# A four-layer kernel on one core: the first stage's closing in another order, middle row tiles written out, bfloat16 bias parts

## The reference

```python
x = x + time_mixing(layernorm(x))      # 16 heads of 8, a scan over the tokens: S = d*S + k v
x = x + top1_ffn(layernorm(x))         # 8 experts 128 -> 512 -> 128 with ReLU, one expert for each token
x = x + memory(layernorm(x))           # holographic memory, below
x = x + top4_moe(layernorm(x))         # 32 experts 128 -> 64 -> 128 and a shared one

# memory: quaternions, 32 of 4 components in 128 channels
keys = (x @ Wk.T + bk).reshape(B, L, 32, 4);  keys = keys / max(norm(keys), 1e-12)
values = (x @ Wv.T + bv).reshape(B, L, 32, 4)
memory = cumsum(quat_mul(values, keys), axis=1)
retrieved = quat_mul(memory, conj(keys)) / sqrt(positions)
return x + (normalize(retrieved) * ln_g + ln_b) @ Wo.T + bo
```

## Time and profile before

| | |
|---|---|
| median of 3 runs | 786.58 us (785.86 to 790.19) |
| the profiled execution | 793.46 us, of which 791.7 from first to last instruction |
| mean granted TensorE clock | 0.977 of full |
| PE busy | 723.0 us (91%) |
| DVE, ACT, POOL busy | 595.1, 485.0, 490.5 us |

### The profile page before, as it was taken

How to read it: one execution, slowest core, us unless ns; L and a number is a source line. 1 busy time by engine, 2 the same in 40 slices (tenths; PEclk the granted TensorE clock), 3 DMA queues, 4 the chain that set the end, 5 groups by cost and what they waited for, 6 DMA issues and landing times.

```text
span 791.7 us, 14395 instructions
## 1 busy us (share of the span) xinstructions
PE 723.0 (91%) x4028; PEld 546.7 (69%) x4029; DVE 595.1 (75%) x1387; ACT 485.0 (61%) x1045; POOL 490.5 (62%) x498
## 2 busy tenths in 40 slices
PE   4999999999868789788999898999999999999996
PEld 2445555455438689777887876787878787878784
DVE  3699999999975645547888777686868686868673
ACT  3677767664535357466566566666666666666553
POOL 3687768787753544447877846555556666555663
PEclk9999999999968999899999999999999999999998
DMA  8800000000011256221000018373636464636550
GB/s 254 253 0 1 2 1 13 9 8 15 14 34 48 55 164 163 68 60 33 14 1 1 2 36 181 72 158 81 150 86 144 95 136 99 131 87 145 112 117 14
DMA packets 38298, 60.48 MB, mean 76 GB/s; under 512 B 3808, under 2 KB 17760, under 8 KB 37840
## 3 DMA queue, kind: packets, MB, share of 16 engines
q1 hardware_dynamic: 35952, 54.94, 29.3%
q0 software_dynamic: 2272, 4.67, 1.7%
HBM read 51.32 MB, written 8.28 MB: 75 GB/s over the span
## 4 chain that ended last, share of the span: by engine, by line
PE 43%; DVE 6%; ACT 2%; issue 2%; DMA 1%; SPq 0%; POOLq 0%; DVEq 0%; POOL 0%; ACTq 0%
PE c_r L1964 3%; PE c_m L1983 3%; PE c_m L1984 3%; PE c_m L1985 3%; PE c_m L1948 3%; PE c_v L1983 2%; PE c_r L2033 2%; PE c_k L1983 2%; PE c_r L2035 2%; PE c_r L2032 2%; PE c_v L1985 2%; PE c_v L1984 2%; PE c_k L1984 2%; PE c_k L1985 2%; PE c_o L2035 2%
## 5 line engine op out<-in xcount | busy, mean ns | idle before, releaser
L2527 POOL TENSOR_TENSOR d_hid_lo<-c_bound,d_hid_hi 128x512 fp32r<-128x512 f32 x136 | 175.5, 1292 | 128.4 <-ACT d_hid_hi L2431 127.0
L2431 ACT ACTIVATE d_hid_hi<-c_bound 128x512 fp32r<-128x512 f32 x136 | 85.4, 628 | 28.1 <-DVE c_bound L2292 26.5
L1471 POOL TENSOR_TENSOR ducts_and_memory_weights<-a_r,state_and_wide 128x512 f32<-128x512 f32 x64 | 75.4, 1189 | 26.7 <-DVE state_and_wide L871 22.2
L871 DVE TENSOR_TENSOR_SCAN state_and_wide<-a_decay,state_and_wide,a_vb 128x512 f32<-128x512 f32 x64 | 80.9, 1266 | 0.4 <-issue 0.3
L2280 DVE TENSOR_TENSOR c_m<-c_bound,c_m 128x512 f32<-128x512 f32 x64 | 44.3, 692 | 23.9 <-PE c_m L1985 17.4
L2280 DVE TENSOR_TENSOR c_v<-c_bound,c_v 128x512 f32<-128x512 f32 x64 | 44.3, 693 | 22.9 <-PE c_v L1985 16.9
L1983 PE MATMUL c_m<-d_x_hi,d_hi 128*128 128x512 f32 x136 | 55.5, 408 | 1.8 <-DVE c_bound L2292 1.8
L2421 ACT ACTIVATE c_bound<-c_m 128x512 f32<-128x512 f32 x60 | 35.8, 596 | 33.3 <-PE c_m L1985 32.8
L2421 ACT ACTIVATE c_bound<-c_k 128x512 f32<-128x512 f32 x60 | 35.8, 597 | 32.8 <-PE c_k L1985 32.2
L1984 PE MATMUL c_m<-d_x_lo,d_hi 128*128 128x512 f32 x136 | 53.9, 396 | 0.0
L1985 PE MATMUL c_m<-d_x_hi,d_lo 128*128 128x512 f32 x136 | 53.9, 396 | 0.0
(11 more groups left out here) (394 smaller groups left out, 2148.3 us busy)
## 6 DMA issues: line engine op xcount, KB each, us to landing
state_and_wide<-pair_weights SPq DMA_DIRECT2D x62, 512.0 KB, 11.7
b_w<-in_w SPq DMA_DIRECT2D x2, 2048.0 KB, 11.6
state_and_wide<-in_moe SPq DMA_DIRECT2D x16, 204.0 KB
a_xf<-rows_in SPq DMA_DIRECT2D x39, 64.5 KB
state_and_wide<-results SPq DMA_DIRECT2D x8, 256.0 KB, 3.1
out<-c_read SPq DMA_DIRECT2D x8, 256.0 KB, 2.4
a_weights<-in_mixing SPq DMA_DIRECT2D x1, 1077.0 KB, 6.6
state_and_wide<-pair_weights SPq DMA_DIRECT2D x2, 384.0 KB, 6.1
```

Of the source, the lines that this page charges most:

```text
L871: dve.tensor_tensor_scan(state[:, j, seq_cols(h, 1)], decay[:, h, :], vb[j % 3][:, :], first, ALU.mult, ALU.add).then_inc(scan_ready, 1)
L1471: pool.tensor_tensor(rs[:, j, :], rr[:, h, :], state[:, j, seq_cols(h, 0)], ALU.mult).then_inc(rs_ready, 1)
L2431: act.activation(hid_hi[:, n % HALVES, :], hidden[:, r, :], ACT.Copy).then_inc(hi_ready, 1)
L2527: pool.tensor_tensor(hid_lo[:, n % HALVES, :], hidden[:, r, :], hid_hi[:, n % HALVES, :].bitcast(F32), ALU.subtract).then_inc(lo_ready, 1)
```

## The change

Four things are altered.

1. `closing` has another order on TensorE, VectorE, ScalarE and GpSimd. The calls are the same.
2. The loop of 16 rows is gone. Rows 12 to 26 (`MIDDLE_ROWS` = 15) are written out, and the written-out rows with steps beside them are the last 12 instead of the last 11. `FIRST_ROWS` is 27 in place of 28. The weights still come in 16 pieces.
3. The steps beside the last rows are given by a table for each engine. ScalarE's normalization of tile 0 is in two halves, and some of its steps come behind the last row.
4. The bias of the projections is held in three bfloat16 parts, on partitions 0, 32 and 64 of 96. In `project` the wait for the turned input stands behind the bias matmul.

```diff
-LOOPED_ROWS = 16
+MIDDLE_ROWS = 15
+PIECES = 16
-FIRST_ROWS = EARLY_ROWS + LOOPED_ROWS
+FIRST_ROWS = EARLY_ROWS + MIDDLE_ROWS
...
-            bodies = LOOPED_ROWS // 8
-            with engine.Fori(0, bodies) as b:
-                for n in range(STORES):
-                    row(STORES * b + EARLY_ROWS + n, (EARLY_ROWS + n) % STORES, b + (EARLY_ROWS + n) // STORES)
+            for k in range(EARLY_ROWS, EARLY_ROWS + MIDDLE_ROWS):
+                row(k, k % STORES, k // STORES)
...
+            def project(bank, name, weight, turned, turned_ready, count):
                 pe.matmul(bank[:, :].rearrange("p (s c) -> p s c", s=SUB), ones[:, :], bias_row(name), start=True, stop=False)
+                pe.wait_ge(turned_ready, count)
...
     (each call of project had its wait for xt_ready or normedt_ready in front of it)
...
-            "bias": ctx.enter_context(nc.sbuf_tensor("bias", [2 * LO_ROW, len(BIASES) * P], F32R)),
-            "ones": ctx.enter_context(nc.sbuf_tensor("ones", [2 * LO_ROW, P], F32R)),
+            "bias": ctx.enter_context(nc.sbuf_tensor("bias", [BIAS_ROWS, len(BIASES) * P], BF16)),
+            "ones": ctx.enter_context(nc.sbuf_tensor("ones", [BIAS_ROWS, P], BF16)),
...
                 if n == 1:
                     dve.wait_ge(bias_rounded, 1)
+                    rest(second, bias_rounded)
+                    rest(third, bias_rounded)
+                if n == 2:
+                    dve.wait_ge(bias_rounded, 3)
+                    rounded_part(second, bias_rounded)
+                    rounded_part(third, bias_rounded)
+                if n == 3:
+                    dve.wait_ge(bias_rounded, 5)
+                    rest(third, bias_rounded)
+                    dve.wait_ge(bias_rounded, 6)
+                    rounded_part(third, bias_ready)
...
-        BESIDE = ((), (), ((0, 3), (0, 4)), ((0, 5), (0, 6), (1, 3), (1, 4)), ((0, 9), (1, 5)), ((0, 12), (1, 6)),
-                  (0, 1), (2, 3), (5,), (6, 7), ((1, 9),))
+                start(norm, ahead, row, {7: [("norm", 0, 12)], 9: [("ahead", 0, 0)]})                      # PE
+                start(norm, ahead, row, {4: [("norm", 0, 3), ("norm", 0, 4)], 5: [("norm", 0, 5), ("norm", 1, 3)],
+                                         6: [("norm", 1, 4)], 7: [("norm", 1, 5)], 10: [("ahead", 0, 2)],
+                                         11: [("ahead", 0, 5), ("ahead", 0, 6)]})                          # DVE
+                start(norm, ahead, row, {6: [("norm", 0, 9)], 7: [("norm", 0, 10)], 8: [("norm", 0, 12)],
+                                         10: [("ahead", 0, 1)], 11: [("ahead", 0, 3)]})                    # ACT
+                start(norm, ahead, row, {5: [("norm", 0, 6)], 7: [("norm", 1, 6)]})                        # POOL
...
             last_rows["act"](beside)
+            ahead(0, 0, 5)
+            ahead(0, 0, 7)
+            norm(1, 1, 9)
             norm(1, 1, 12)
```

More of the change, by code:

```diff
@@ L432, in emit @@
             def emit(beside):
-                for k in range(EARLY_ROWS + LOOPED_ROWS, ROW_TILES):
+                for k in range(EARLY_ROWS + MIDDLE_ROWS, ROW_TILES):
                     row(k, k % STORES, k // STORES)
-                    beside(k - EARLY_ROWS - LOOPED_ROWS)
+                    beside(k - EARLY_ROWS - MIDDLE_ROWS)
                 if end:
@@ L1137, in closing @@
                 e0 = bias_hidden(0, 0, 0)
+                e1 = bias_hidden(1, 1, 0)
+                tail(7, 1, 11)
+                look(6, 0, 8)
+                pick(5, 1, 13)
+                pick(5, 1, 14)
+                e2 = bias_hidden(2, 2, 0)
+                look(6, 0, 9)
                 tail(7, 1, 13)
-                pick(6, 0, 13)
-                pick(6, 0, 14)
-                e1 = bias_hidden(1, 1, 0)
+                bias_out(0, 0, e0)
+                e3 = bias_hidden(3, 3, 0)
                 tail(7, 1, 15)
@@ L1144, in closing @@
                 look(7, 1, 2)
-                e2 = bias_hidden(2, 2, 0)
-                look(7, 1, 8)
-                look(7, 1, 9)
-                bias_out(0, 0, e0)
-                e3 = bias_hidden(3, 3, 0)
                 bias_out(1, 1, e1)
                 e4 = bias_hidden(4, 4, 0)
+                look(7, 1, 8)
+                pick(6, 0, 8)
+                look(7, 1, 9)
+                pick(6, 0, 9)
+                pick(6, 0, 10)
+                pick(6, 0, 11)
                 bias_out(2, 2, e2)
+                pick(6, 0, 13)
+                pick(6, 0, 14)
                 e5 = bias_hidden(5, 5, 0)
+                bias_out(3, 3, e3)
+                e6 = bias_hidden(6, 6, 0)
+                bias_out(4, 4, e4)
                 pick(7, 1, 8)
@@ L1365, in closing @@
             def closing():
+                pick(5, 1, 5)
                 act.wait_ge(early_loaded, 16 * (len(early) + 4))
@@ L1516, in closing @@
                 send_one(7, 3)
-                give_back(3, 3)
                 give_back(4, 4)
@@ L1713, in bias_row @@
             n = BIASES.index(name)
-            return bias[:, n * P:(n + 1) * P].unsqueeze(1).broadcast_to([2 * LO_ROW, SUB, P])
+            return bias[:, n * P:(n + 1) * P].unsqueeze(1).broadcast_to([BIAS_ROWS, SUB, P])
         def spread_component(ap):
@@ L1793, in split_cols, with start @@
             return n, slice(part * width, (part + 1) * width)
-        BESIDE = ((), (), ((0, 3), (0, 4)), ((0, 5), (0, 6), (1, 3), (1, 4)), ((0, 9), (1, 5)), ((0, 12), (1, 6)),
-                  (0, 1), (2, 3), (5,), (6, 7), ((1, 9),))
-        def start(norm, ahead, row):
-            for each in BESIDE[row]:
-                if isinstance(each, tuple):
-                    norm(each[0], each[0] % 2, each[1])
+        def start(norm, ahead, row, places):
+            for stage, i, step in places.get(row, ()):
+                if stage == "norm":
+                    norm(i, i % 2, step)
                 else:
-                    ahead(0, 0, each)
+                    ahead(i, i % 2, step)
         def weave(engine, norm, ahead, main, tail, look, route, unit, end):
@@ L2073, in beside @@
                     pe.wait_ge(loaded["taken"], 1)
-                start(norm, ahead, row)
+                start(norm, ahead, row, {7: [("norm", 0, 12)], 9: [("ahead", 0, 0)]})
             last_rows["pe"](beside)
@@ L2322, in norm @@
             def norm(i, h, step):
-                if step == 9:
+                if step in (9, 10) and (step == 9 or i == 0):
                     act.wait_ge(shift_ready, i + 1)
@@ L2326, in norm @@
                     need(act, kept_ready, i - 1)
-                    for s in range(SUB):
+                    for s in range(SUB) if i else (0, 1) if step == 9 else (2, 3):
                         a = act.activation(xn[:, h, s, :], x_tok[:, SUB * i + s, :], ACT.Identity,
                                            bias=shift[:, s:s + 1], scale=rstd[:, s:s + 1])
-                    a.then_inc(xn_ready, 1)
+                    if i or step == 10:
+                        a.then_inc(xn_ready, 1)
                 if step == 12:
@@ L2443, in beside @@
                     act.wait_ge(loaded["taken"], 1)
-                start(norm, ahead, row)
+                start(norm, ahead, row, {6: [("norm", 0, 9)], 7: [("norm", 0, 10)], 8: [("norm", 0, 12)],
+                                         10: [("ahead", 0, 1)], 11: [("ahead", 0, 3)]})
             last_rows["act"](beside)
+            ahead(0, 0, 5)
+            ahead(0, 0, 7)
+            norm(1, 1, 9)
             norm(1, 1, 12)
@@ L2534, in beside @@
                 if row == 3:
-                    pool.wait_ge(bias_ready, 1)
+                    pool.wait_ge(bias_rounded, 1)
                     pool.wait_ge(loaded["taken"], 1)
-                start(norm, ahead, row)
+                start(norm, ahead, row, {5: [("norm", 0, 6)], 7: [("norm", 1, 6)]})
             last_rows["pool"](beside)
@@ L2618, in packed_quaternions @@
     part["wo"][:] = t["Wo"].T
-    for row in (0, LO_ROW):
+    for row in range(0, BIAS_ROWS, PART_ROWS):
         part["bias"][row] = np.concatenate([t[name] for name in BIASES])
```

186 lines of the change are left out of this document (85 added, 101 removed).

## The result

The changed kernel takes 775.52 us (773.95 to 777.01) where the kernel before took 786.58: 0.9848 of it, interval 0.9821 to 0.9875. Timed twice more beside the kernel before it gave 0.9844 (0.9828 to 0.9860) and 0.9869 (0.9851 to 0.9887). The forecast was 764 with a range of 757 to 775. The sign was right and the size was half: 10.8 to 12.7 us of the 22.7.

The account below looks back on a forecast made before the run. TensorE was taken to bound the looped rows and memory stage, with waits of about 8 to 9 us in each stretch beside the rows. Gains 7 + 3.3 + 6.3 + 6.1 = 22.7 us off 786.58 gave 764 us, range 757 to 775.

Parts of the forecast that it names:

- closing: End of the first stage: reordering brings row 12's bias about 6 us behind the plan, not 15.2; 7 us gained.
- rows written out: Rows 12 to 26 without the loop: 1.90 us each on TensorE, 28.5 us instead of 31.76; 3.3 us gained.
- head: Last rows with the memory stage's start: VectorE's 2.27 us wait for returned results goes; 6.3 us gained, bounds 3 and 9.
- memory stage: Three bias matmuls per tile get cheaper or leave the chain; 6.1 us gained, bounds 3.0 and 8.7.
- I take zero: Closing: the plan itself was assumed to come neither earlier nor later; bounds -2 (gain) and +5 us.
- Rival 1: Closing gives little, 1 us, as the plan slips behind three expands or stalls return; 770 us, chance 0.17.
- value term: Memory stage, value projection: a cheaper bias matmul saves 0.30 us in each of seven tiles.
- output term: Memory stage, output projection: the bias matmul moves into TensorE's wait for normed_t, saving 0.50 us, counted eight times.
- Does TensorE stay the bound? It does: Memory stage: VectorE's work, GpSimd's read and TensorE's reads make 13.3 us per tile, below the 14.0 forecast.
- rival 2: Written-out rows: instructions come late, at most three stalls, +10 us on the forecast, 774 us; chance 0.08.
- rival 3: The 96-row bias matmul is no cheaper and the head's wait moves: memory part 3, head 3, 770 us; chance 0.08.
- Rivals 4 and 5: 4: waits re-form everywhere, 785 us, chance 0.04. 5: lower clock stays through written-out rows, 792.5 us, chance 0.03.

Follow-up runs that it names:

- middle_only: The kernel before with its 16 looped rows written out and nothing else; 784.18 us, 0.9970 of before.
- closing_back: The changed kernel with the old order of the closing on all four engines; 778.36 us, 0.9889 of before.
- after_again: The changed kernel unaltered, run once more for a trace at the ordinary TensorE clock; 774.16 us.
- after_third: The changed kernel unaltered, run once more on the chip of the third group; 776.61 us, 0.9869 of before.
- head_back: The changed kernel with the steps beside the last rows at their old places, FIRST_ROWS still 27; 794.04 us, 1.0026 of before, on the second group's chip.
- bound_first: The changed kernel with VectorE's two products (bound) ahead of the addition got in the memory stage; 770.3 us, 0.9784 of before.
- norm_early: The changed kernel with VectorE's results' addition and statistics of memory tiles 3 to 7 half a tile earlier; 792.73 us, 0.9999 of before, second group's chip.

## Why the prediction was right in sign and wrong in size

| term | forecast | measured |
|---|---|---|
| closing | 7 | 1.0 alone, 1.75 in company |
| rows written out | 3.3 | 2.65 alone; 1.7 and 3.1 in the traces (31.76 to 30.10 and 28.66) |
| head | 6.3 | 4.8 to 6.0 in the traces (38.70 to 33.88 and 32.71); no run timed it alone |
| memory stage | 6.1 | 1.5 by the medians, 2.9 in the traces |

**Closing: the step that failed is "I take zero" for the plan, and the 15.2 us before it.** That row 12 would come about 6 us behind the plan was right (6.70, 7.64). But the new order makes the plan later: it ends at 265.8 and 266.4, in the old order, on chips of the same sort, at 261.8, 262.9 and 262.7. I had looked for that at `tail(7, 14)` behind three expands, and it isn't there: the last addition to x is at 244.55 against 243.99 in middle_only. The loss comes behind it, 16.1 us from there to the plan's start in place of 12.7 (13.6 in closing_back). Read from the order of time (no run tested it), two places make up most of the difference. The turning of tile 7's rows (`pick(7)` 4) stands on TensorE behind `contract(3)` and `expand(6)` and starts at 252.62, 1.85 us after they are ready, where in middle_only it is 0.63. `bias_hidden(8)` and `bias_out(5)`, which I had counted as work taken from behind the plan, stand before it: VectorE is done with tile 7's index at 259.16 and starts the plan at 260.69, where in middle_only it starts it at once. `count_all`, now behind `expand(8)`, ends at 258.5 and holds up nothing. What is taken from one side of a fixed piece is put on the other. And the 15.2 us held stalls of that chip: the order itself gives 12.0 to 12.3. From there to the 6.7 to 7.9 with the new order are 4 to 5 us, and the plan, 3 to 4.6 us later, takes most of them. Rival 1 named this outcome (closing 1 us) with the wrong place; its 770 is not the result, since a second term failed too.

**Rows: right where they run free.** In after_again six steps from 291.25 to 302.62 are 1.90 us each and the clock is 1.00, but the rows before them take longer (one step, where TensorE waits for a row's load, is 3.20), so that the 15 steps are 30.10 us; in after_third and middle_only they are 28.66, close to the 28.5 of the forecast. Alone the part gives 2.65 and not 3.3.

**Head: right, place by place in the trace.** The wait for the results went, that for `shift` is 2.53, TensorE's 2.66. The bias parts held the addition to 10.2 us behind row 27, where I had 8.6, and ScalarE's start came at 16.5 for 15.4; later steps gave it back. (The forecast's terms for the aggregates add up to 11.6, where it has 12.0.) How much of it is the new places stays open between 1.4 and 3.6 us, by head_back.

**Memory stage: the value term was right, the output term 0.43 for 0.50, and waits took back 0.47.** The value bias is 0.22 us to the next start and the eight behind it 0.89: 1.11 us from the bias to `c_m`, where the order in time of before has 0.42 and 0.99, so 0.30. The Trainium skill's TensorEngine Tiling (Array Packing), Key Properties, has the engine drained when the tiling mode changes; it doesn't say to which mode a 96-row matmul belongs, and the trace is what one would see if it were that of the 128-row ones. Rows and number type changed together, but the 512 columns of the earlier trace rows, float32r on 128 rows, are 0.23 us apart, so the 0.42 does not come of the type. From ScalarE's start to the output weights it is 0.83 us where the order in time of before has 1.26 (the chain of the earlier trace rows has 1.33), so 0.43, the lower bound. But then TensorE meets VectorE. `c_r` starts 1.16 us after `c_o` and not 0.99. The key bias is 0.21 us shorter too, and `c_m` starts 1.49 us after the key weights and not 1.19, with 0.43 of waiting for `bound`. That is 0.30 + 0.43 + 0.21 less 0.17 and 0.30, or 0.47; and the step is 14.33 us, where before had 14.70 and 14.92 in turn: 0.48 less, not 0.80. (The upper bound of 8.7 has no terms beside it; eight times 0.50 and 0.39 are 7.1.) The step that failed is "Does TensorE stay the bound? It does", with a floor of 13.3: I followed GpSimd's read and left out the ring read, `got`, `bound`, `c_m`. bound_first cuts the ring with one exchange and gives 1.0 us a tile, which shows that the ring held the step.

**Instructions late (rival 2).** On two chips it is nothing: no idle time without a releaser in eight profiles. The Trainium skill's Runtime: NRT & Kernel Launch, Instruction fetch mechanics, calls sequential fetching mostly hidden, and those traces agree. On the chip of the second group the stalls of the variants are up to 8.35 us in code without a jump, and they eat the whole gain. Whether they are instructions coming late is not shown: in norm_early the DMA view has no instruction packet between 268 and 277 us, when both engines stand. It stays open, as does the changed kernel's own time on such a chip.

**The other rivals.** The 96-row bias was cheaper, against rival 3, though the memory stage gave no more than the 3 us that it had for it. Rivals 4 and 5 are out: the time fell by 1.3 to 1.6%, and the clock, which was to stay low in the written-out rows, was 1.00 there.

## What to carry to other kernels

A gain read as "the distance behind a fixed piece of work" has to be booked on both sides of the piece: ask what the moved work now delays. When an instruction gets shorter on the engine that sets the pace, look which other engine it meets next; a ring through another engine's order (take up, then produce) was undone here by swapping two independent steps. And take the profile of before on more than one chip before a stall in it is given a price.

## What the runs showed of the hardware

VectorE's clamp of 128x128 took 0.23 us in norm_early, and 1.19 us in after_again, where it begins 0.15 us behind a GpSimd addition of 512 columns and ends 0.07 us after it:

```profile
412.18 1.27 POOL L2488 TENSOR_TENSOR c_kept<-c_xn,x_tok 128x512 f32<-128x512 f32 x1
...
412.33 1.19 DVE L2121 TENSOR_SCALAR c_norm_max<-c_length 128x128 f32<-128x128 f32 x1
```

The Trainium skill's SBUF — State Buffer, SBUF: two separate sides, has VectorE and GpSimd share a pair of ports: of a GpSimd instruction and a VectorE one that needs the pair too, the one that starts first holds it for a whole instruction and the other is blocked. The trace agrees: in a later tile of after_again the clamp begins 0.04 us ahead of the addition (426.47 and 426.51) and takes 0.20. I had priced VectorE's way without it, with the long clamp as it stood.

And one kernel differs by 0.8% between the chips of the first and second group (786.8 and 793.2 us), nearly all of it behind 240 us: the old closing brings row 12's bias at 274 to 275 us on the chips of the first and third group and at 281.1 on that of the second.
